# Expert output products as three passes over split halves of the activations and of w2, one tile behind

## What is computed

```
# layer 0: one expert per token, ReLU
h = relu(x @ W1[e] + b1[e])          # 256 -> 1024
y = h @ W2[e] + b2[e]                # 1024 -> 256
out = gate(token) * y                # e = argmax of the router

# layer 1: two experts per token, gated
h = silu(x @ w1[e].T) * (x @ w3[e].T)
out += weight(token, e) * (h @ w2[e].T)
```

## Time and profile before

| what | value |
|---|---|
| median of 3 runs | 1735.67 us (1729.64 to 1739.29) |
| the profiled execution, its own time | 1732.06 us |
| span of the profiled execution | 1730.2 us |
| PE busy | 1479.9 us (86%) |
| DVE busy | 832.5 us (48%) |
| ACT busy | 522.7 us (30%) |
| POOL busy | 417.6 us (24%) |
| first products of expert stage 0 to its last store issue | 325.98 to 501.2 us |
| the same of expert stage 1 | 973.34 to 1398.3 us |

### The profile page before, as it was taken

How to read it: one execution, slowest core, us unless ns; L and a number is a source line. 1 busy time by engine, 2 the same in 40 slices (tenths; PEclk the granted TensorE clock), 3 DMA queues, 4 the chain that set the end, 5 groups by cost and what they waited for, 6 DMA issues and landing times. The chain is left out here.

```text
span 1730.2 us, 31832 instructions
## 1 busy us (share of the span) xinstructions
PE 1479.9 (86%) x11282; PEld 1285.6 (74%) x11282; DVE 832.5 (48%) x2319; ACT 522.7 (30%) x1300; POOL 417.6 (24%) x651
## 2 busy tenths in 40 slices
PE   4789986599958999999994599999999978985775
PEld 3466664489957888888884599999999967864664
DVE  4677663322215666666665311111111127876996
ACT  1233332112214445445441111111111112334553
POOL 2011101133223444433322100000000036730222
PEclk7799999699989999999997699999999989996888
DMA  7655420783410000000000444224426232100000
GB/s 149 109 92 107 76 38 20 271 272 107 132 40 20 7 13 14 20 19 14 7 8 13 162 170 170 97 97 170 170 95 244 85 98 68 50 6 1 13 13 25
DMA packets 99469, 141.90 MB, mean 82 GB/s; under 512 B 10209, under 2 KB 83425, under 8 KB 99233
## 3 DMA queue, kind: packets, MB, share of 16 engines
q1 hardware_dynamic: 81968, 111.92, 22.3%
q0 software_dynamic: 6368, 18.62, 3.7%
q10 hardware_dynamic: 11024, 9.97, 1.9%
HBM read 113.22 MB, written 14.42 MB: 74 GB/s over the span
## 5 line engine op out<-in xcount | busy, mean ns | idle before, releaser
L1603 PEld LDWEIGHTS f_ph<-f_xgT,f_w 128*128 128x128 f32 x3232 | 374.0, 194 | 10.5 <-issue 4.2
L1603 PE MATMUL f_ph<-f_xgT,f_w 128*128 128x128 f32 x3232 | 375.3, 277 | 5.3 <-DMA f_w<-in_f_w 2.7
L1613 PE MATMUL f_py<-f_w,f_hT 128*128 128x256 f32 x992 | 224.7, 379 | 0.2 <-ACT f_hT L1645 0.2
L1613 PEld LDWEIGHTS f_py<-f_w,f_hT 128*128 128x128 f32 x992 | 183.6, 190 | 23.3 <-issue 0.8
L1677 DVE TENSOR_TENSOR f_hT<-f_ph,f_gate_o 128x512 f32<-128x512 f32 x78 | 53.9, 691 | 262.9 <-ACT f_gate_o L1639 262.9
L1576 POOL DMA_INDIRECT f_xg<-normed_x,order x62 | 59.5, 960 | 498.8 <-PE f_px L1592 464.2
L987 ACT ACTIVATE a_work<-a_ps,a_bias 128x128 f32<-128x128 f32 (+1 forms) x256 | 104.1, 419 | 172.5 <-issue 98.0
L1187 POOL TENSOR_TENSOR a_work<-a_work,a_recip 128x256 f32<-128x256 f32 (+1 forms) x128 | 103.2, 828 | 147.8 <-DVE a_recip L1106 146.7
L1639 ACT ACTIVATE f_gate_o<-f_ph 128x512 f32<-128x512 f32 x78 | 46.6, 597 | 295.2 <-PE f_ph L1603 295.1
L574 DVE CUSTOM_DVE_ANT_0 a_shut_s<-a_ps,a_neg 128x256 f32<-128x256 f32 x256 | 93.0, 419 | 39.5 <-PE a_ps L253 39.0
L486 ACT ACTIVATE a_pT<-a_ps 128x1024 f32<-128x1024 f32 x64 | 65.5, 1024 | 118.8 <-PE a_ps L253 118.8
(11 more groups left out here) (319 smaller groups left out, 2881.0 us busy)
## 6 DMA issues: line engine op xcount, KB each, us to landing
f_w<-in_f_w SPq DMA_DIRECT2D x70, 1024.0 KB, 7.8
sorted_y<-f_yg ACTq DMA_DIRECT2D x62, 128.0 KB, 1.7
a_qs<-a_part SPq DMA_DIRECT2D x48, 128.0 KB, 4.4
a_ks<-a_part SPq DMA_DIRECT2D x42, 128.0 KB, 6.2
normed_x<-a_xn SPq DMA_DIRECT2D x16, 256.0 KB, 2.1
x<-in_x SPq DMA_DIRECT2D x8, 256.0 KB, 6.6
a_mask<-in_mask SPq DMA_DIRECT2D x8, 256.0 KB, 6.4
a_maskT<-in_maskT SPq DMA_DIRECT2D x8, 256.0 KB, 6.5
```

The costliest lines, as they stand in the source:

```text
L1603: mm = pe.matmul(ph[:, q, n, f * P:(f + 1) * P], w[:, s, k, (q * FQ + f) * P:(q * FQ + f + 1) * P], xgT[:, s, k, :], start=(k == 0), stop= ...
L1613: mm = pe.matmul(py[:, s, 0:D], hT[:, s, f, :], w2[:, s, f, :], start=(f == 0), stop=(f == FT - 1))
```

## The change

In both expert stages the output product is now made like those of attention 1: the activated rows `h` are split into a high part, which is h rounded to float32r, and a low part, the rest; w2 likewise; and `py` sums high by high, high by low and low by high, all float32r. Nothing else of what is computed changes.

- ACT and DVE write h to a single buffer `raw`. ACT copies each half of it into `h_high` (`hidden_high`, 512 columns), and DVE subtracts this from `raw` into `h_low` (`hidden_low`).
- For every tile, also where the expert stays the same, ACT copies the whole w2 of the tile into `w2_high` (`weights_high`, 2048 columns), at the start of the tile, once the weights are there and output product i - 2 is done. DVE then subtracts it from w2 into `w2_low` (`weights_low`, 2048 columns).
- PE does the output product of tile i - 1 behind the products with w1 of tile i and the transposes of tile i + 1; for the last tile both follow each other. DVE's `take_out` and ACT's `store` of tile i - 1 stand accordingly at the end of tile i.
- In stage 0 DVE reads the expert of the tile twice per tile (in `finish` and in `take_out`), before once.
- SP starts w1 and w3 at the end of the products with w1 of tile i - 2, and w2 when `w2_low` of tile i - 2 is made.
- The two `raw` buffers of `split_weights` now lie in `xt`, to make room.
- All engines run tile 0 in front of a loop of four tiles, and the last two behind it.

```diff
-    raw = [ctx.enter_context(nc.sbuf_tensor("a1_raw%d" % n, [P, DK * H64], F32)) for n in range(2)]
+    raw = [spare[:, n, :] for n in range(2)]
...
-        hT = sb("hT", [P, 2, FT, P])
+        raw = sb("raw", [P, Q, FQ * P])
+        hT = [sb("h_" + n, [P, 2, FT, P], F32R) for n in ("high", "low")]
+        w2_parts = [sb("w2_" + n, [P, 2, FT, D], F32R) for n in ("high", "low")]
...
+        def tiles(engine, body):
+
+            body(0, 0, 0, first=True)
+            with engine.Fori(0, (NT - 3) // 4) as four:
+                for j in range(1, 5):
                     body(four * 4 + j, j % 2, four * 2 + j // 2)
-            for i in range((NT - 1) // 4 * 4, NT - 1):
-                body(i, i % 2, i // 2)
-            body(NT - 1, (NT - 1) % 2, (NT - 1) // 2, last=True)
-
-        def every_tile(engine, body):
-
-            with engine.Fori(0, NT // 2) as pair:
-                body(pair * 2, 0, pair)
-                body(pair * 2 + 1, 1, pair)
-            if NT % 2:
-                body(NT - 1, 0, NT // 2)
+            body(NT - 2, 1, (NT - 3) // 2)
+            body(NT - 1, 0, (NT - 1) // 2, last=True)
...
-                sp.wait_ge(turned, i + 2)
+                sp.wait_ge(h_ready, i * 2 - 2)
...
-                    sp.wait_ge(y_ready, i + 1)
+                    sp.wait_ge(w2_low, i - 1)
...
+            def output(i, s):
+                pe.wait_ge(h_low, i * 2 + 2)
+                pe.wait_ge(w2_low, i + 1)
+                pe.wait_ge(y_out, i + 1)
+                for f in range(FT):
+                    for n, (a, b) in enumerate(PASSES):
+                        mm = pe.matmul(py[:, s, 0:D], hT[a][:, s, f, :], w2_parts[b][:, s, f, :],
+                                       start=(f == 0 and n == 0), stop=(f == FT - 1 and n == len(PASSES) - 1))
+                mm.then_inc(y_ready, 1)
+
+            def multiply(i, s, half, first=False, last=False):
+                hidden(i, s, half)
                 if not last:
                     turn(i + 1, 1 - s, half + s)
-                pe.wait_ge(y_out, i + 1)
-                for q in range(Q):
-                    pe.wait_ge(h_out[q], i + 2)
-                    for f in range(q * FQ, (q + 1) * FQ):
-                        mm = pe.matmul(py[:, s, 0:D], hT[:, s, f, :], w2[:, s, f, :],
-                                       start=(f == 0), stop=(f == FT - 1))
-                mm.then_inc(y_ready, 1)
+                if not first:
+                    output(i - 1, 1 - s)
+                if last:
+                    output(i, s)
 
             turn(0, 0, 0)
-            tiles_but_last(pe, multiply)
+            tiles(pe, multiply)
...
+            def weights_high(i, s, half):
+                act.wait_ge(w_ready[s], (half + 1) * (16 * NW))
+                act.wait_ge(y_ready, i + 1)
+                act.activation(w2_parts[0][:, s, :, :], w2[:, s, :, :], ACT.Copy).then_inc(w2_high, 1)
+
+            def hidden_high(i, s, q):
+                act.wait_ge(h_out[q], i + 2)
+                act.activation(hT[0][:, s, q * FQ:(q + 1) * FQ, :].rearrange("p f n -> p (f n)"), raw[:, q, :], ACT.Copy
+                               ).then_inc(h_high, 1)
+
+            def store(i, s):
+                act.wait_ge(y_out, i + 3)
+                act.dma_start(ys[bass.ds(i * P, P), :], yg[:, s, :]).then_inc(stored[s], 16)
+
+            def gate(i, s, half, first=False, last=False):
+                weights_high(i, s, half)
                 if gated:
                     for q in range(Q):
                         act.wait_ge(h_ready, i * 2 + (q + 1))
                         act.wait_ge(h_out[q], i + 1)
                         act.activation(gate_o[:, q, :], ph[:, q, 0, :], ACT.Silu).then_inc(gate_done, 1)
+                        if q == Q - 1 and not last:
+                            turn_out(i + 1, 1 - s)
+                        hidden_high(i, s, q)
                 else:
                     e = act.value_load(table[0:1, bass.ds(i + 2, 1)], min_val=0, max_val=E - 1)
                     act.wait_ge(h_ready, i * 2 + 1)
-                    act.wait_ge(y_ready, i + 1)
+                    if not first:
+                        act.wait_ge(h_low, i * 2 - 1)
                     for f in range(FQ):
-                        a = act.activation(hT[:, s, f, :], ph[:, 0, 0, f * P:(f + 1) * P], ACT.Relu,
+                        a = act.activation(raw[:, 0, f * P:(f + 1) * P], ph[:, 0, 0, f * P:(f + 1) * P], ACT.Relu,
                                            bias=b1[:, e, f:f + 1])
                     a.then_inc(h_out[0], 1)
-                if not last:
-
-                    act.wait_ge(h_ready, i * 2 + 1)
-                    turn_out(i + 1, 1 - s, half + s)
-                act.wait_ge(y_out, i + 3)
-                act.dma_start(ys[bass.ds(i * P, P), :], yg[:, s, :]).then_inc(stored[s], 16)
+                    hidden_high(i, s, 0)
+                    if not last:
+                        turn_out(i + 1, 1 - s)
+                    hidden_high(i, s, 1)
+                if not first:
+                    store(i - 1, 1 - s)
+                if last:
+                    store(i, s)
 
             act.sem_inc(stored[0], 16)
             act.sem_inc(stored[1], 16)
-            turn_out(0, 0, 0)
-            tiles_but_last(act, gate)
+            turn_out(0, 0)
+            tiles(act, gate)
...
+            def weights_low(i, s):
+                dve.wait_ge(w2_high, i + 1)
+                dve.tensor_tensor(w2_parts[1][:, s, :, :], w2[:, s, :, :], w2_parts[0][:, s, :, :], ALU.subtract
+                                  ).then_inc(w2_low, 1)
+
+            def hidden_low(i, s, q):
+                dve.wait_ge(h_high, i * 2 + (q + 1))
+                dve.tensor_tensor(hT[1][:, s, q * FQ:(q + 1) * FQ, :].rearrange("p f n -> p (f n)"), raw[:, q, :],
+                                  hT[0][:, s, q * FQ:(q + 1) * FQ, :].rearrange("p f n -> p (f n)"), ALU.subtract
+                                  ).then_inc(h_low, 1)
+
+            def take_out(i, s, half):
+                if not gated:
                     e = dve.value_load(table[0:1, bass.ds(i + 2, 1)], min_val=0, max_val=E - 1)
-                    dve.wait_ge(h_ready, i * 2 + 2)
-                    dve.wait_ge(y_ready, i + 1)
-                    for f in range(FQ):
-                        a = dve.tensor_scalar(hT[:, s, FQ + f, :], ph[:, 1, 0, f * P:(f + 1) * P],
-                                              b1[:, e, FQ + f:FQ + f + 1], 0.0, ALU.add, ALU.max)
-                    a.then_inc(h_out[1], 1)
                 dve.wait_ge(y_ready, i + 3)
                 dve.wait_ge(stored[s], half * 16 + 16)
                 if gated:
                     dve.tensor_copy(yg[:, s, :], py[:, s, 0:D]).then_inc(y_out, 1)
                 else:
                     dve.tensor_tensor(yg[:, s, :], py[:, s, 0:D], b2[:, e, :], ALU.add).then_inc(y_out, 1)
-            every_tile(dve, finish)
+
+            def finish(i, s, half, first=False, last=False):
+                weights_low(i, s)
+                if gated:
+                    for q in range(Q):
+                        dve.wait_ge(gate_done, i * 2 + (q + 1))
+                        if not first:
+                            dve.wait_ge(h_low, i * 2 + (q - 1))
+                        dve.tensor_tensor(raw[:, q, :], ph[:, q, 1, :], gate_o[:, q, :], ALU.mult).then_inc(h_out[q], 1)
+                        hidden_low(i, s, q)
+                else:
+                    e = dve.value_load(table[0:1, bass.ds(i + 2, 1)], min_val=0, max_val=E - 1)
+                    dve.wait_ge(h_ready, i * 2 + 2)
+                    if not first:
+                        dve.wait_ge(h_low, i * 2)
+                    for f in range(FQ):
+                        a = dve.tensor_scalar(raw[:, 1, f * P:(f + 1) * P], ph[:, 1, 0, f * P:(f + 1) * P],
+                                              b1[:, e, FQ + f:FQ + f + 1], 0.0, ALU.add, ALU.max)
+                    a.then_inc(h_out[1], 1)
+                    hidden_low(i, s, 0)
+                    hidden_low(i, s, 1)
+                if not first:
+                    take_out(i - 1, 1 - s, half + (s - 1))
+                if last:
+                    take_out(i, s, half)
+
+            tiles(dve, finish)
```

More of the change, by code:

```diff
@@ L666, in _, with split_weights @@
                     take_out(i, 1)
-def split_weights(nc, ctx, io):
+def split_weights(nc, ctx, io, spare):
     H64 = H * D1
@@ L1492, in _, with expert_tiles @@
             mm.then_inc(ordered, 1)
-def expert_tiles(nc, top, tag, xs, ys, table, order, NT, io, consts, weights, gated, meanwhile=None, ahead=None, beside=None):
+def expert_tiles(nc, top, tag, xs, ys, table, order, NT, io, consts, weights, gated,
+                 meanwhile=None, ahead=None, beside=None):
     NW = 3 if gated else 2
@@ L1501, in expert_tiles @@
     FQ = FT // Q
+    PASSES = ((0, 0), (0, 1), (1, 0))
     with top.stage() as ctx:
@@ L1514, in expert_tiles @@
```

(32 more changed lines are left out.)

10 lines of the change are left out of this document (1 added, 9 removed).

## The result

The changed kernel takes 1740.93 us (median of 20 runs, 1734.65 to 1752.28), the kernel before 1735.8 us beside it (20 runs). The ratio estimated from all runs is 1.0043, with a 95% interval from 1.003 to 1.0055 (the two medians alone give 1.0030): **slower, by 0.4%**, where the forecast was faster by 0.7%. The time lies inside the stated range, and the difference is about as small as the 0.5% that the prediction counted as no change, but its sign is settled by the interval. The profiled execution has its own time of 1736.80 us, 4.7 over that of before (1732.06).

What follows compares the result with a forecast made beforehand. PE's own work was taken to bound both expert stages before; after, an ACT-DVE chain bounds stage 0. 11.4 + 1 + 1 - 23.1 = -9.7 us, from 1732.06 to 1722.4; predicted 1724, range 1706 to 1750.

Steps and rivals of the forecast that it cites:

- The step that failed: Stage 0: POOL's splitting of the attention weights, 1.04 or 2.37 us in 16 tiles, has free time; 1 us added.
- the ring: Stage 0: take-out, store, w2 copy, subtraction, ReLU, splitting run once per tile, 8.0 us against PE's 6.62; +11.4 us.
- Rival B: Stage 0: POOL and DVE hinder each other at two-SBUF-input subtractions, adding 12 us, 27 at worst; 1734 to 1749; chance 0.12.
- PE's gain: Both expert stages: 24 float32r products take 2.83 us instead of 3.46 for 16 float32 records, 0.63 us less per tile.
- rival E: Output products, both stages: three passes not cheaper, 4.8 us each, some 80 us more, 1815; or a lower clock; chance 0.04.
- Rival D: Stage 0: overlapping DVE subtractions make the per-tile chain shorter, 7.5 us, giving 1712; chance 0.13.
- Stage 1 stays PE-bound: Stage 1: PE's 10.19 us per tile exceeds the 9.67 us chain through ACT and DVE; -23.1 us.
- rival C: Stage 1 bound by its ACT and DVE chain too, 10.9 us per tile, 27 us back; halfway 1738; chance 0.14.
- The table's readings: Stage 0: DVE reads the expert twice per tile, up to 0.77 us each, mostly hidden behind running subtractions.
- Rival A: Stage 0: DVE's readings of `table` lengthen the per-tile chain to 9.5 us, 33 us more, 1747 to 1756; chance 0.13.
- PE's waits for weights: Stage 0: earlier loads hide the 2.7 us of waits, except about 1 us at tiles 2 and 3.
- What ends PE's wait: Stage 0: PE waits 1.4 us per tile for DVE's ReLU of half 1 or the low part of h.

Runs made afterwards that it cites:

- the first kernel of the experiments: Against the changed kernel, POOL's attention-weight splitting piece for tile i waits for the take-out of tile i - 4; 1727.73 us, 0.9961 of before.

## Why the prediction was wrong

**The step that failed** is this one: "POOL's splitting of the attention weights, 1.04 or 2.37 us in 16 tiles, has free time; I add 1 us for it." It cost 15.4 us by the stretched instructions and some 12 us by the run that moved it. POOL did have free time. DVE did not, and it was DVE that was stopped, inside the ring that bound the stage. Without this term's error the sum would have been near: 11.4 + 1 + 15.4 - 23.1 = +4.7 us against 4.7 measured between the profiled executions. The last agreement is luck: stage 1 gained 1.9 us less than summed, and against that stand 1.8 us that came ahead of stage 0, where nothing was changed, and smaller differences.

Rival B named the mechanism, the place and 12 us, and got a chance of 0.12. Its estimate let the two meet by chance: a busy share of DVE times POOL's 27 us. They don't meet by chance. PE's transposes release POOL's gather, and POOL's piece follows it (393.11, 393.76, 394.73 above); the take-out releases ACT's copy of w2 and that the subtraction (392.19, 393.31, 395.26). In a tile bound by the ring both chains start at about the same time, so POOL's subtraction starts about half a microsecond ahead of DVE's in five of its eight tiles, and in the other three it meets DVE all the same. What spoke for B was all in hand: the subtractions stood in the ring, so any stretch of them would be paid in full, and the two chains could have been laid on one time axis.

The Trainium skill, "GPSIMD Engine Reference", section "Key points", was quoted for this rival: GpSimd contends with VectorE instructions that have two SBUF inputs. The trace agrees, and adds the size: DVE loses nearly the overlap, 1.75 of 1.87 us in the tile shown, and each of the ten stretched instructions the overlap less 0.12 to 0.14 us.

**The other steps, in their order.**
- PE's gain: 0.63 us per tile was predicted, 0.58 is measured in stage 1, whose tile is 10.24 us instead of 10.82. From the first of the 24 output products to the next product with w1 are 2.95 us there, where 2.83 was predicted. Over 38 tiles the 0.05 us are 1.9, the whole gap between -21.2 and -23.1. Right, and rival E falls: the products are cheaper and the granted clock in stage 0 is 0.98 (0.99 before). There is one stretch of low clock in it: after PE was busy for 9.1 of the 13 us to 443, it has 0.72 in the mean from 443 to 449 us, and 32 products' records take 5.44 us (443.03). The take-outs there are as far apart as in the same tiles of the other turns of the loop, so it costs nothing.
- The ring: 7.7 to 8.0 us where it is undisturbed (8.4 once per turn of the loop), 8.07 on average in the run with POOL's pieces moved; 8.0 was predicted. Right, with the 2.29 us taken for the subtraction. With POOL's pieces out of the way stage 0 still takes 2 us more than the sum gave: 188.9 - 174.5 = 14.4 us where 11.4 + 1 was predicted. Rival D falls.
- Stage 1 stays PE-bound. Right; rival C falls.
- The table's readings: 0.23 us per tile for the one that was taken out. Rival A falls.
- PE's waits for weights: 2.7 us, as before, where the prediction let them hide but for about 1 us. Too low by 1.7 us at most, which changes nothing in the verdict.
- What ends PE's wait: I had named DVE's ReLU of half 1 or the low part of h. It is the copy of `xgT` on ACT (24.3 of 32 us), which is queued behind ACT's copy of w2 and its ReLU. The same ring, entered at another point.

## What to carry to other kernels

When a change puts pieces on two engines, write the chain through both as a ring with its waits and compare it with what the bound engine needs per tile. Here 8.0 against 6.6 us told that the stage would be bound by it, and one order closed it: a copy that could go ahead of a store stood behind it. Moving the copy gave 32 us, more than the 26.8 us that the stage had lost.

Before calling an engine's work free, ask not only whether that engine has time, but whose instructions it lies beside, and whether those are on the path. Lay the releases of both on one time axis: two pieces that the same tile releases keep their distance from tile to tile, so they can meet nearly every time (here all eight of POOL's subtractions) or never (in the kernel that moved them), and not in proportion to their shares.

Making work smaller that is off the path gains nothing, as the two kernels that split w2 only 27 times show.

## What the runs showed of the hardware

**When a DVE subtraction with both inputs in SBUF and POOL meet, one of them stands still, and it can be either.** The Trainium skill, "SBUF — State Buffer", section "SBUF: two separate sides", says that of such a pair of instructions the one that starts first keeps the shared ports and the other blocks. In the ten meetings of the changed kernel POOL's piece came first and DVE was stopped, which agrees. POOL's pieces with one input (the copy) stop DVE as its subtractions do.

POOL's gathers show the other side. Order of time after, DVE and POOL:

```profile
448.90 2.29 DVE L1702 TENSOR_TENSOR f_w_low<-f_w,f_w_high 128x2048 fp32r<-128x2048 f32 x1 [2.63 <-ACT f_w_high L1644]
448.96 3.06 POOL L1573 DMA_INDIRECT f_xg<-normed_x,order  x1 [8.44 <-PE f_px L1589]
```

DVE starts first and takes its 2.29 us; the gather, 0.95 us elsewhere, takes 3.06 and ends 0.83 us behind DVE's end. In the first kernel of the experiments this happens ten times: the gathers take 1.17 to 3.05 us, and each ends 0.82 to 0.89 us behind DVE's end. That agrees with the Trainium skill as well. It also moves the piece behind the gather: here POOL's subtraction starts at 452.03 and so meets the pair for h.

In a few places a piece of POOL starts in the middle of DVE's instruction, and it is still DVE that is longer. In the kernel with stage 0 alone changed, and then in the kernel with the early copy, order of time:

```profile
359.68 0.97 POOL L1573 DMA_INDIRECT f_xg<-normed_x,order  x1 [3.58 <-PE f_px L1589]
360.19 3.67 DVE L1702 TENSOR_TENSOR f_w_low<-f_w,f_w_high 128x2048 fp32r<-128x2048 f32 x1 [2.59 <-ACT f_w_high L1644]
360.66 1.05 POOL L696 CAST a_wq_high<-xt 128x1024 fp32r<-128x1024 f32 x1
```

```profile
352.17 0.96 POOL L1573 DMA_INDIRECT f_xg<-normed_x,order  x1 [5.92 <-PE f_px L1589]
353.01 3.70 DVE L1709 TENSOR_TENSOR f_h_low<-f_raw,f_h_high 128x512 fp32r<-128x512 f32 x2
...
353.14 2.41 POOL L699 TENSOR_TENSOR a_wq_low<-xt,a_wq_high 128x1024 fp32r<-128x1024 f32 x1
```

These do not contradict what the Trainium skill says there, because POOL was not idle when DVE started: its gather was running, and the piece followed at once. DVE's loss counts the gather too. At 360.19 it is 1.38 us, more than the whole 1.05 us of the copy, and equal to the 1.51 us beside gather and copy less 0.13, as in the other meetings. A gather with no piece behind it does not stop DVE: in the first kernel of the experiments one runs from 432.97 for 0.97 us, and the subtraction that starts at 433.34 takes 2.29 us. Why the gather counts in the one case and not in the other stays open, and no run here has a piece of POOL that starts in the middle of DVE's subtraction with POOL idle ahead of it.

**A source in PSUM is not hit.** After, in attention 1, first DVE's order of time, then POOL's:

```profile
572.35 0.42 DVE L1066 TENSOR_TENSOR a_o_low<-a_ps,a_o_high 128x256 fp32r<-128x256 f32 x1
572.69 0.68 DVE L1098 COPY a_V<-a_ps 128x512 f32<-128x512 f32 x1
...
571.94 1.61 POOL L1187 TENSOR_TENSOR a_work<-a_work,a_recip 128x256 f32<-128x256 f32 x2
```

DVE's subtraction at 572.35 lies wholly beside POOL's work, but one of its inputs comes from PSUM, and it takes 0.42 us, as the same instruction does where POOL is idle (0.42 us, 50 times). ACT isn't hit either: its copy of h, from SBUF to SBUF, takes 0.63 us beside POOL and without it.
